# Routed experts beside a recurrence on one core: one cast moved to ACT, plan steps dropped, statistics moved in DVE's order, another bank for the last tile's transposes

## What is computed

```python
xn = layernorm(x)
# branch s: two complex linear recurrences over the 256 tokens, then a gate
b_i = (xn @ W_re_i + b_re_i + 1j*(xn @ W_im_i + b_im_i)) * (1 - r_i)
h_i = real(scan(h_t = a_i * h_{t-1} + b_t))              # a_i fixed
h = concat(h_0, h_1);  s = sigmoid(h @ W_gate + b_gate) * h
# branch g: each token goes to the best 2 of 8 experts
top2, w = top_k(xn @ Wg + bg, 2), softmax of the two logits
y_e = (silu((w*xn) @ W1[e]) * ((w*xn) @ W3[e])) @ W2[e]   # 128 -> 512 -> 128
g = silu(xn + y of the two chosen experts)
out = x + s * g
```

## Time and profile before

| | |
|---|---|
| median of 3 runs | 315.67 us (315.18 to 317.34) |
| the profiled execution | 315.75 us |
| its span from first to last instruction | 314.0 us |
| outside the span | 1.75 us |
| PE busy | 289.3 us (92%) |
| DVE busy | 230.4 us (73%) |
| ACT busy | 171.0 us (54%) |
| POOL busy | 149.1 us (47%) |

### The profile page before, as it was taken

How to read it: one execution, slowest core, us unless ns; L and a number is a source line. 1 busy time by engine, 2 the same in 40 slices (tenths; PEclk the granted TensorE clock), 3 DMA queues, 4 the chain that set the end, 5 groups by cost and what they waited for, 6 DMA issues and landing times.

```text
span 314.0 us, 6542 instructions
## 1 busy us (share of the span) xinstructions
PE 289.3 (92%) x1973; PEld 255.7 (81%) x1973; DVE 230.4 (73%) x614; ACT 171.0 (54%) x361; POOL 149.1 (47%) x172
## 2 busy tenths in 40 slices
PE   8885795999999999999999998999999999997983
PEld 8774754899987989889998888999999999786331
DVE  3898887998598795768776785786776777574086
ACT  2889557576255975466646654455455554442031
POOL 2448878677114666376656742234344343334010
PEclk9955599999999999999999999999999999999998
DMA  6959714036210151112419649759786834940696
GB/s 188 348 174 324 224 49 145 29 90 181 70 33 20 42 153 51 36 43 69 109 52 154 181 126 352 247 194 319 263 287 243 312 99 151 335 133 13 226 382 195
DMA packets 42797, 52.17 MB, mean 166 GB/s; under 512 B 5622, under 2 KB 33530, under 8 KB 40844
## 3 DMA queue, kind: packets, MB, share of 16 engines
q1 hardware_dynamic: 36428, 40.57, 41.8%
q0 software_dynamic: 4320, 8.43, 8.1%
q10 hardware_dynamic: 2016, 2.76, 2.5%
HBM read 22.20 MB, written 14.26 MB: 116 GB/s over the span
## 4 chain that ended last, share of the span: by engine, by line
PE 65%; DVE 13%; issue 6%; ACT 6%; DMA 4%; POOL 2%; SPq 1%; POOLq 0%; DVEq 0%
PE bank L1485 12%; PE bank L1429 5%; PE bank L1438 5%; PE bank L1431 5%; PE bank L1430 5%; PE bank L1469 4%; PE bank L1440 4%; PE bank L1439 4%; PE bank L1486 4%; PE bank L1220 3%; PE bank L1221 3%; PE bank L1222 3%; PE bank L1531 3%; DMA early<-in_L_attn_x 3%; PE bank L1405 2%
## 5 line engine op out<-in xcount | busy, mean ns | idle before, releaser
L551 POOL DMA_INDIRECT y_dram<-stage,row x71 | 69.5, 978 | 104.4 <-DVE stage L1153 89.9
L542 POOL DMA_INDIRECT rows_dram<-rows,slot_row x64 | 68.4, 1068 | 25.3 <-issue 15.0
L735 ACT ACTIVATE stage<-bank 128x512 f32<-128x512 f32 x71 | 42.4, 598 | 69.4 <-PE bank L1431 40.2
L1485 PE MATMUL bank<-ew,hid_t 128*128 x284 | 73.0, 340 | 1.3 <-DVE stage L1153 0.7
L1485 PEld LDWEIGHTS bank<-ew,hid_t 128*128 128x128 f32 x284 | 53.4, 188 | 1.7 <-issue 1.6
L748 ACT ACTIVATE hid_t<-bank 128x512 fp32r<-128x512 f32 x71 | 40.8, 598 | 10.6 <-PE bank L1469 7.9
L1137 DVE TENSOR_TENSOR stage<-bank,stage 128x512 f32<-128x512 f32 x41 | 28.1, 686 | 17.5 <-PE bank L1431 17.0
L1429 PE MATMUL bank<-ew,row_t_hi 128*128 x82 | 34.6, 422 | 4.7 <-DVE row_t_lo L1131 4.5
L1486 PE MATMUL bank<-ew,hid_t 128*128 x164 | 36.4, 222 | 0.0
L1137 DVE TENSOR_TENSOR bank<-bank,stage 128x512 f32<-128x512 f32 x30 | 21.0, 699 | 17.8 <-PE bank L1440 17.7
L1431 PE MATMUL bank<-ew,row_t_hi 128*128 x82 | 32.3, 394 | 0.0
(11 more groups left out here) (178 smaller groups left out, 703.4 us busy)
## 6 DMA issues: line engine op xcount, KB each, us to landing
u<-ew SPq DMA_DIRECT2D x10, 1024.0 KB, 5.0
mix<-ew SPq DMA_DIRECT2D x5, 1024.0 KB, 5.5
stage<-in_L_ffn_W SPq DMA_DIRECT2D x15, 256.0 KB, 4.9
early<-in_L_attn_x SPq DMA_DIRECT2D x7, 512.0 KB, 4.8
row<-rows_dram SPq DMA_DIRECT2D x41, 64.5 KB, 2.0
xn_dram<-early SPq DMA_DIRECT2D x4, 512.0 KB, 4.0
u<-xn_dram SPq DMA_DIRECT2D x4, 512.0 KB
ew<-y_dram SPq DMA_DIRECT2D x8, 256.0 KB, 6.9
```

Source lines behind the costliest of these rows:

```text
L542: pool.indirect_dma_start(out=rows_dram[:, :], out_offset=bass.IndirectOffsetOnAxis(ap=slot_row[:, q % 2, at:at + 1], axis=0), in_=rows[:, ...
L551: pool.indirect_dma_start(out=y_dram[:, :], out_offset=bass.IndirectOffsetOnAxis(ap=row[:, k, D:ROW].bitcast(U32), axis=0), in_=y[:, t % Y ...
L735: act.activation(silu[:, t % 2], bank[:], ACT.Silu).then_inc(silu_done, 1)
L1485: pe.matmul(to, hi[:, at:at + P], w[c], start=(c == 0), stop=False, skip_group_check=True)
```

## The change

1. The high parts of expert 5 are made by ACT, between `weights_hi(3)` and `turning_weight(1)`, and no longer by DVE between the routing steps of group 1. So that PE can wait for the two experts separately, `w_hi_laid` becomes a list of two semaphores.
2. `planning_step` leaves out step 3 for phase 0 and step 4 for phases 0 to 3; step 5 then reads the tile that the skipped steps would have passed on.
3. At tile 0 DVE's `spread(0)` stands behind `multiplied(0)`, two small steps and `row_lo(1)`.
4. `turned_bank(55)` is bank 4, the bank that the rows were transposed into, and `transpose_hidden(55)` waits for one `hidden_lo` fewer.

```diff
@@ semaphores
-        w_hi_laid, lay_ready, w_laid = sem("w_hi_laid"), sem("lay_ready"), sem("w_laid")
+        w_hi_laid, lay_ready, w_laid = [sem(f"w_hi_laid{n}") for n in range(len(LAID))], sem("lay_ready"), sem("w_laid")
@@ turned_bank(j)
-            return banks[7] if j == FIRST_PAIR - 1 else turning(j)[1]
+            return banks[7] if j == FIRST_PAIR - 1 else banks[4] if j == J - 1 else turning(j)[1]
@@ ACT weights_hi(e)
-                               ACT.Copy).then_inc(w_hi_done, 1)
+                               ACT.Copy).then_inc(w_hi_laid[LAID.index(e)] if e in LAID else w_hi_done, 1)
@@ ACT, the order before the tiles
             weights_hi(3)
+            weights_hi(5)
             turning_weight(1)
             weights_hi(6)
@@ DVE weights_hi(e)
-                                ).then_inc(w_hi_laid, 1)
+                                ).then_inc(w_hi_laid[LAID.index(e)], 1)
@@ DVE planning_step(g, n)
+                if (g == 0 and n == 3) or (g < LONE and n == 4):
+
+                    return
...
-                    then(dve.tensor_copy(avail[:], units_i[:]))
+                    then(dve.tensor_copy(avail[:], (tiles_i if g == 0 else left_i if g < LONE else units_i)[:]))
@@ DVE, the order before the tiles
                 routing(1, n)
-            weights_hi(5)
             weights_hi(7)
@@ DVE, the loop over tiles
-                spread(t)
+                if t:
+                    spread(t)
...
                     if j + 1 < J:
                         row_lo(j + 1)
+                    if t == 0:
+
+                        spread(t)
                     small_step(t, 1)
@@ PE low_parts(e)
-                pe.wait_ge(w_hi_laid, n + 1)
+                pe.wait_ge(w_hi_laid[n], 1)
@@ PE transpose_hidden(j)
-                pe.wait_ge(hidt_lo_done, t)
+
+                pe.wait_ge(hidt_lo_done, t if j < J - 1 else t - 1)
```

## The result

The changed kernel takes 315.26 us as the median of 22 runs (314.27 to 316.19), the kernel before 316.14 us in 22 runs beside them: a ratio of 0.9968, 95% interval [0.9958, 0.9977], that is 1.0 us less [0.7, 1.3]. The forecast was 1.05 us less (as an absolute time 314.6 us, taken from the first three runs of the kernel before, whose median was 315.67). Each ratio in this document compares only those executions of a kernel that are within 1.5% of its fastest. The total was right; the way to it was not the one that I had written for the front, as the traces show. One execution of the changed kernel was profiled: 315.36 us, span 313.6 us, 0.4 us less than the span before.

The account below looks back on a forecast made before the run. PE, busy for 92% of the span, was taken as the bound, so other engines' savings count only where the chain leaves it. 315.75 - 0.25 (front) - 0.80 (last tiles) = 314.70 us, median forecast 314.6, range 312.9 to 316.0.

Parts of the forecast that it names:

- the front: 31 to 57 us, from the expert casts and first plan to PE's `up(2)`; claimed to give 0.25 us altogether.
- Part 4, 0.80 us: Last tiles: `transpose_hidden(55)` starts 0.80 us sooner behind `down(53)`, and all 0.80 us reaches the last scatter.
- Part 1, 0: Expert 5's cast fits ACT's idle time, 1.7 us to spare; DVE only waits longer for PE's mixing: gain 0.
- Part 2, 0.25 us at `row_hi(0)`: First plan 0.38 us shorter, but ACT's preceding `weights_laid(7)` lets `row_hi(0)` gain only 0.25 us; later phases 0.
- Part 3, given back behind ACT: `up(1)` 1.75 us sooner, but ACT's eight rows and `h_hi(0)` gain only 0.25; 1.5 us returns as PE idle time.
- The front's 0.25 us as a whole: 31 to 57 us: `up(2)` starts at 56.6 instead of 56.85, the first three edits together giving 0.25 us.
- Rival 1: Tile 0's moved statistics pay their full 1.75 us because ACT does not bind: 313.1 us; chance 0.13.
- Rivals 2 and 3: Second: front gives nothing, `row_hi(0)` stays near 48.06, 314.9 us, chance 0.12. Third: end gives nothing, 315.4 us, chance 0.07.
- Rival 5: PE's clock rises later during the mixing, making the kernel slower; 5 us later gives 316.6 us; chance 0.05.
- rule weighed ahead of the result: PE's clock during the mixing: the chip's activity look runs free of the kernel, so the rise shifts between runs.

Follow-up runs that it names:

- part 4 alone: The kernel before, with only the last tile's transposes moved to bank 4 and waiting for one `hidden_lo` fewer: 315.18 us, ratio 0.9984 [0.9968, 1.0001].

## Why the prediction was right, and where it was wrong

- **Part 4, 0.80 us: right.** 0.79 us in the pair of traces, the same 5.53 us against 6.32 or 6.33 in every trace with and without it. It is more than the 0.4 us by which the two spans differ.
- **Part 1, 0: right where I looked, not elsewhere.** The cast ran at 32.68 with 1.70 us to spare. DVE's idle time ahead of the placement did not grow to the 1.7 us that I named but to 1.27, because the mixing ended sooner. What I did not foresee is the late product near 142 us, which costs 0.2 us in every trace with part 1; its cause is open.
- **Part 2, 0.25 us at `row_hi(0)`: right for the pair of traces, not a fixed amount.** From the end of the mixing to `row_hi(0)` it is 7.77 us before and 7.51 after (0.26 less). But with part 4 alone, which has the long plan, it is 7.50: there the row's load went out 5.12 us behind the end of the mixing (5.43 before), and PE turned the row round without waiting for it, where before it waited 0.45 us. So the term is 0 to 0.26 us in these traces, by whether the row lands late.
- **Part 3, given back behind ACT: right in its direction, and the step that failed is inside it.** I wrote that ACT's eight rows and `h_hi(0)` have no idle time among them and "gain 0.25 only", with `h_hi(0)` at 52.92. It came at 53.14. The rows have a wait of their own, for the landing of group 0's last scatter, which I had left out: in the trace of before it was just met (the rows began 0.18 us behind the start of the second row's high part), so no row named it. I moved ACT's work by 0.25 us without asking whether what was ready just in time would be ready sooner. It was not, it became later: DVE's subtractions, moved forward by the plan, held the scatter up. I named no queue on POOL but that of `rstd`, and wrote that no DMA changed its place; a scatter's place had not changed, its length had.
- **The rule that bears on it.** The Trainium skill (SBUF — State Buffer, section "Who interferes with whom") says that a DVE instruction with two SBUF inputs contends with a GpSimd instruction that reads SBUF. The kernel before already showed it, in the next scatter's 3.06 us, and the runs here agree: 3.47 to 4.34 us under the two subtractions, 0.96 us when these are cut to a twelfth. That it is the second input that does it rests on the Trainium skill; no run here isolates it.
- **The front's 0.25 us as a whole: not confirmed.** It is 0.05 in the pair of traces, with a clock that rose 0.88 us sooner for the changed kernel; measured against the mixing's end it is 0.35 worse. By the median parts 1 to 3 give 0.4 us [-0.2, 1.0] without part 4. An estimate from the changed kernel's own ratio: 1.0 us [0.7, 1.3], less 0.79 of the end, plus 0.21 lost near 142 us, leaves 0.4 us [0.1, 0.7] for the front and all that varies. So the sum was right with a right large term; that the small terms, one of them a loss I had not named, come to nearly what I had written is in part luck. Their mean over many executions was not measured term by term.
- **Rival 1** (the statistics pay in full): false, and false also once ACT is out of the way, which I had not foreseen. **Rivals 2 and 3**: the front's trace looks like rival 2, the end's does not look like rival 3. **Rival 5**, the clock: the rise does move, but over 36.7 to 38.9 us, and it moves the end of the mixing by 1.08 us (39.32 to 40.40), as large as the whole effect in one execution. That it averages out in the medians is likely and not shown. The prediction also gives two chances to a time beyond rival 1, 0.03 in the split of the forecast and 0.06 in the sentence on 312.5 us; these do not agree.

## What to carry to other kernels

Where a step is advanced, look not only at what it waits for in the trace but at what its engine's next instructions wait for and find met just in time: such a wait has no row, and it is the next bound. A long VectorE subtraction with two SBUF inputs beside a scatter that POOL issues was a cost here as soon as somebody waited for that scatter; moving the waiting work (here eight rows on ACT, spread over four tiles, 1.8 us in all against 1.0) gave more than trimming the steps ahead of it. And an edit of 0.3% cannot be read off one pair of traces: stretches far from the edits differ by 0.4 us between them. Nor is such a difference all chance: half of it came with one of the edits in every trace, which only the other kernels' traces could show.

## What I had not expected of the hardware

- The step of PE's clock from the lower level to full speed lay anywhere between 36.71 and 38.87 us in ten traces with the same PE work ahead of it, starting at 33.6 to 33.8 us. The Trainium skill's rule weighed ahead of the result (TensorE: Matmul & The Clock Gate, "What's actually happening") holds in that the rise is not tied to an instruction; its spread here, 2.16 us from first to last, is wider than the ±0.5 us that this section of the Trainium skill gives.
- A scatter on POOL that starts 0.39 us behind the start of DVE's first subtraction (44.23 and 43.84), or 0.1 us ahead of it, does not get through between the two subtractions either, though they are two instructions: it ended 0.8 us behind the second one.
- The clock can also fall near the end: in one trace it was granted at 0.50 for the stretch of 301 to 303 us, behind 2 us in which PE was busy for 0.80, and the last matmuls took 1.69 us longer; in another trace PE was busy for 0.70 there and the clock stayed at 1.00.
- A chip can be 8% slower on this kernel (342 us beside 316) with the same 1,973 matmuls: PE is busy for 297 to 301 us in place of 289 and stands still for 1 to 4 us in several places. What causes this was not looked into.
